# A decoder step in one kernel: one group's shift divided between ACT and POOL, eight squares moved a layer forward, TensorE's idle products in two batches, the last eight rows normed by DVE

## The reference

```
x = layernorm(x + scan(x))             # gates, values = sigmoid, tanh of x @ W.T + b; hidden = gate*hidden + value
x = layernorm(x + ssm(ctx, ctx, x))    # products of context channels, convolved over 128 tokens, times x
x = layernorm(x + routed(x))           # 8 experts: score, best gate, low-rank update
x = layernorm(x + causal_attention(x))
x = layernorm(x + cross_attention(x, ctx))   # quantised weights, self and cross heads
x = layernorm(x + mixture(x))          # 8 experts, the 2 best of each token
```

```
x_diff = x_diff / norm(x_diff)
score  = sum((select_weight . x_diff) ** 2)
gate   = sigmoid(slope * (score - center))        # best expert by the largest gate
out    = (1 - gate) * x + gate * (bias + degen . (update . (x - debias)))
```

## Time and profile before

| | |
|---|---|
| median of 3 runs | 1453.36 us (1452.62 to 1458.38) |
| the profiled execution's own time | 1458.62 us |
| its span, first to last instruction | 1456.9 us |
| mean granted TensorE clock | 0.969 of full |
| busy | PE 93%, DVE 73%, ACT 64%, POOL 60% |
| front block | 0 to 145 us |
| routed block | 145 to 189 us |
| causal attention block | from 189 us |
| last adds landed, rows loaded, normed, stored | 1435.5 us to the end |

### The profile page before, as it was taken

How to read it: one execution, slowest core, us unless ns; L and a number is a source line. 1 busy time by engine, 2 the same in 40 slices (tenths; PEclk the granted TensorE clock), 3 DMA queues, 4 the chain that set the end, 5 groups by cost and what they waited for, 6 DMA issues and landing times. The chain is left out here.

```text
span 1456.9 us, 27654 instructions
## 1 busy us (share of the span) xinstructions
PE 1353.1 (93%) x8289; PEld 1099.2 (75%) x8306; DVE 1060.7 (73%) x2549; ACT 938.7 (64%) x3150; POOL 877.0 (60%) x1052
## 2 busy tenths in 40 slices
PE   9998878895799999999999999999999988999992
PEld 4445656663489999999988888888888856888881
DVE  4898748896788888888988788887788856333332
ACT  3996447775578787888887777777776645222222
POOL 3896127774077676776886756756657622555543
PEclk9999789998999999999999999999999989999996
DMA  9321110000101001010010100100001175333334
GB/s 344 140 116 58 35 45 1 2 2 1 44 2 45 1 1 56 1 49 5 23 62 2 45 1 2 45 1 2 1 1 34 41 249 163 52 52 52 53 47 126
DMA packets 46085, 72.77 MB, mean 50 GB/s; under 512 B 4044, under 2 KB 32660, under 8 KB 43636
## 3 DMA queue, kind: packets, MB, share of 16 engines
q1 hardware_dynamic: 37028, 51.86, 10.5%
q0 software_dynamic: 7488, 10.23, 4.3%
q10 hardware_dynamic: 1424, 8.91, 1.5%
HBM read 50.94 MB, written 20.05 MB: 49 GB/s over the span
## 5 line engine op out<-in xcount | busy, mean ns | idle before, releaser
L1783 ACT ACTIVATE pr_<-ps,neg_ 128x128 f32<-128x128 f32 x512 | 180.9, 365 | 73.4 <-DVE neg_ L1900 72.6
L1841 POOL TENSOR_TENSOR rstd<-var,half 128x6 f32<-128x6 f32 x128 | 172.3, 1346 | 10.1 <-POOL var L1836 0.2
L1800 ACT ACTIVATE y<-ps,invsm 128x128 bf16<-128x128 f32 x512 | 145.5, 368 | 25.7 <-PE ps L1714 25.5
L1836 POOL TENSOR_TENSOR var<-stat,deps 128x6 f32<-128x6 f32 x128 | 25.2, 197 | 224.8 <-DVE stat L1880 224.8
L1852 POOL TENSOR_TENSOR z<-t,m 128x512 fp32r<-128x512 f32 x128 | 148.6, 1161 | 1.7 <-DVE t L1926 1.7
L1696 PE MATMUL ps<-qkt 128*128 128x128 f32 x1024 | 144.5, 284 | 2.3 <-ACT qkt L1775 2.1
L1696 PEld LDWEIGHTS ps<-qkt 128*128 128x128 f32 x1024 | 124.0, 191 | 29.6 <-issue 26.9
L1725 PE MATMUL ps<-phi,z 128*128 128x256 f32 x512 | 137.9, 301 | 0.7 <-POOL z L1852 0.5
L1845 POOL TENSOR_TENSOR pr_<-pr_,rec_ 128x512 f32<-128x512 f32 x128 | 133.2, 1040 | 3.4 <-DVE rec_ L1907 3.4
L1714 PE MATMUL ps<-XT 128*128 128x256 f32 x512 | 132.1, 380 | 0.6 <-ACT XT L1791 0.6
L1725 PE MATMUL ps<-plo,z 128*128 128x256 f32 x512 | 127.6, 282 | 0.0
(11 more groups left out here) (339 smaller groups left out, 3951.2 us busy)
## 6 DMA issues: line engine op xcount, KB each, us to landing
centred<-raw_weights ACTq DMA_DIRECT2D x8, 1024.0 KB, 3.9
w_low<-w_dram SPq DMA_DIRECT2D x8, 1024.0 KB, 10.4
aw_st<-centred SPq DMA_DIRECT2D x7, 1024.0 KB, 5.0
raw_weights<-wself_dram SPq DMA_DIRECT2D x4, 1024.0 KB, 13.8
raw_weights<-wcross_dram SPq DMA_DIRECT2D x4, 1024.0 KB, 14.5
w<-w_dram SPq DMA_DIRECT2D x2, 2048.0 KB, 19.4
aw_rows<-wproj_dram SPq DMA_DIRECT2D x7, 512.0 KB, 4.0
tz<-toep_dram SPq DMA_DIRECT2D x1, 2048.0 KB, 11.7
```

The source lines that it names most:

```text
L1783: ins = act.activation(pr[:, u.par, h, :], bS[:, h * S:(h + 1) * S], ACT.Exp, bias=neg[:, u.par, h:h + 1], accum_out=tot[:, u.par, h:h + 1])
L1800: ins = act.activation(y[:, u.par, h * S:(h + 1) * S], bO[:, h * S:(h + 1) * S], ACT.Copy, scale=invsm[:, head:head + 1])
L1841: pool.tensor_tensor(rstd[:, u.par, 0:6], v, half[:, :], ALU.pow).then_inc(s_rstd, 1)
```

## The change

Four edits.

- **Shift of n0's group 1.** DVE no longer makes it; it waits for rstd and norms its two rows. ACT makes the group's fall behind the first of the four evacuations of the last group, and POOL makes the shift behind rstd, before the last `borders` and `total(2)`. The function is split into `fallen` and `shifted_by_pool`; for the other groups the instructions stay as they were.
- **Eight squares.** The squares of rows 0 to 7 are done by ACT in the front block, behind the keeping of n1's groups 0 and 1 and before its wait for group 2, with the idle `gate` tile as their unused output. xx moves to the weights object that outlives the block. The routed block keeps rows 8 to 15.
- **Idle products.** 7, a wait for Exp (s_ex), 5 more, then the wait for mk (s_mk). Before it was 8 and then the wait for mk.
- **Last rows.** DVE norms all rows of quarters 2 and 3. ACT makes the falls of quarters 0 and 1 ahead of its rows; POOL makes no fall any more, and a shift only for quarters 0 and 1.

```diff
     def deviations_and_shift(self, pool, power, tg):   # split
+    def fallen_by_act(self, act, tg):
+        g = self.group(tg)
+        act.wait_ge(self.means, 4 * tg + 4)
+        act.activation(self.fall[:, g], self.mean_var[:, g, 0], ACT.Copy, scale=-1.0).then_inc(self.falls, 1)
+    def shifted_by_pool(self, pool, tg):
+        g = self.group(tg)
+        pool.wait_ge(self.falls, self.falling.index(tg) + 1)
         pool.wait_ge(self.rstds, tg + 1)
         pool.tensor_tensor(self.shift[:, g], self.fall[:, g], self.rstd[:, g], ALU.mult).then_inc(self.shifts, 1)
...
                 n0.normed_by_act(act, 0)
-                evacuate(3, range(3))
+                evacuate(3, range(1))
+                n0.fallen_by_act(act, 1)
+                evacuate(3, range(1, 3))
                 n0.normed_by_act(act, 1)
...
                 n1.keep_by_act(act, 1, range(CB))
+                routed.squares(act, lambda b: gate[:, b // 4, b // 2 % 2, b % 2 * C:(b % 2 + 1) * C], X, range(B // 2))
                 n1.normed_by_act(act, 2)
...
                 n0.deviations(pool, power, 1)
+                n0.shifted_by_pool(pool, 1)
                 borders(3)
                 total(2)
...
                 scan(2)
-                n0.shifted(dve, 1)
+                dve.wait_ge(n0.rstds, 2)
                 n0.normed_by_dve(dve, 1)
                 scan(3)
...
+    def squares(self, act, out, X, bs):
+        for b in bs:
+            ins = act.activation(out(b), X[:, b, :], ACT.Square, accum_out=self.xx[:, b:b + 1])
+        return ins
...
-        GROUPS, WIDE, DUMMIES = B // 4, 4, 8
+        GROUPS, WIDE, DUMMIES = B // 4, 4, (7, 5)
...
-                for _ in range(DUMMIES):
-                    pe.matmul(weights.projection(ps, 0)[:, 0:W512], ident[:, :], ident[:, :].unsqueeze(1).to_broadcast([P, 4, P]),
-                              start=True, stop=True)
+                for count, s_next in zip(DUMMIES, (s_ex, s_mk)):
+                    for _ in range(count):
+                        pe.matmul(weights.projection(ps, 0)[:, 0:W512], ident[:, :], ident[:, :].unsqueeze(1).to_broadcast([P, 4, P]),
+                                  start=True, stop=True)
+                    pe.wait_ge(s_next, 1)
...
-                for b in range(B):
-                    ins = act.activation(sq[:, b, :], X[:, b, :], ACT.Square, accum_out=xx[:, b:b + 1])
-                ins.then_inc(s_sq, 1)
+                weights.squares(act, lambda b: sq[:, b, :], X, range(B // 2, B)).then_inc(s_sq, 1)
...
-        by_dve = lambda q: range(4 * q, 4 * q + 2) if q >= QUARTERS // 2 else range(0)
+        by_dve = lambda q: quarter_rows(q) if q >= QUARTERS // 2 else range(0)
...
-                for q in range(QUARTERS):
+                for q in range(QUARTERS // 2):
+                    act.wait_ge(s_mean, q + 1)
+                    act.activation(fall[:, quarter(q)], mean_var[:, quarter(q), 0], ACT.Copy, scale=-1.0).then_inc(s_fall, 1)
+                for q in range(QUARTERS // 2):
                     act.wait_ge(s_shift, q + 1)
...
                     pool.wait_ge(s_mean, q + 1)
-                    pool.tensor_scalar(fall[:, quarter(q)], mean_var[:, quarter(q), 0], -1.0, None, ALU.mult).then_inc(s_fall, 1)
...
+                    if by_act(q):
+                        pool.wait_ge(s_rstd, q + 1)
+                        pool.wait_ge(s_fall, q + 1)
+                        pool.tensor_tensor(shift[:, quarter(q)], fall[:, quarter(q)], rstd[:, quarter(q)], ALU.mult
+                                           ).then_inc(s_shift, 1)
```

More of the change, by code:

```diff
@@ L194, with __init__ @@
 class RowNorm:
-    def __init__(self, tag, shared, pairs, ctx, sem, sbuf, X, XT, ps, ident):
-        self.shared, self.pairs, self.X, self.XT, self.ps, self.ident = shared, pairs, X, XT, ps, ident
+    def __init__(self, tag, shared, falling, pairs, ctx, sem, sbuf, X, XT, ps, ident):
+        self.shared, self.falling, self.pairs, self.X, self.XT, self.ps, self.ident = shared, falling, pairs, X, XT, ps, ident
         self.row_stats = sbuf(ctx, tag + "_row_stats", [P, B, 6], F32)
@@ L250, in deviations_and_shift @@
         pool.tensor_scalar(self.fall[:, g], self.mean_var[:, g, 0], -1.0, None, ALU.mult).then_inc(self.falls, 1)
-        self.deviations(pool, power, tg)
-        pool.wait_ge(self.falls, 1 + sum(t not in self.shared for t in range(tg)))
+    def shifted_by_pool(self, pool, tg):
+        g = self.group(tg)
+        pool.wait_ge(self.falls, self.falling.index(tg) + 1)
         pool.wait_ge(self.rstds, tg + 1)
@@ L362, in front_layer @@
         early = sbuf(ctx, "a_early", [P, 1], F32)
-        n0 = RowNorm("n0", (0, 1), ((4, 5), (6, 7), (0, 1), (4, 5)), ctx, sem, sbuf, X, XT, ps, ident)
-        n1 = RowNorm("n1", (2, 3), ((0, 1), (4, 5), (2, 3), (6, 7)), ctx, sem, sbuf, X, XT, ps, ident)
+        n0 = RowNorm("n0", (0, 1), (1, 2, 3), ((4, 5), (6, 7), (0, 1), (4, 5)), ctx, sem, sbuf, X, XT, ps, ident)
+        n1 = RowNorm("n1", (2, 3), (0, 1), ((0, 1), (4, 5), (2, 3), (6, 7)), ctx, sem, sbuf, X, XT, ps, ident)
         centring = Centring(ctx, sem, sbuf)
@@ L582, in _ @@
                     if n == 3:
-                        n0.deviations_and_shift(pool, power, 2)
+                        n0.fallen(pool, 2)
+                        n0.deviations(pool, power, 2)
+                        n0.shifted_by_pool(pool, 2)
                     if n == 7:
-                        n0.deviations_and_shift(pool, power, 3)
+                        n0.fallen(pool, 3)
+                        n0.deviations(pool, power, 3)
+                        n0.shifted_by_pool(pool, 3)
                     if n == 26:
-                        n1.deviations_and_shift(pool, power, 0)
+                        n1.fallen(pool, 0)
+                        n1.deviations(pool, power, 0)
+                        n1.shifted_by_pool(pool, 0)
                     if n == 28:
-                        n1.deviations_and_shift(pool, power, 1)
+                        n1.fallen(pool, 1)
+                        n1.deviations(pool, power, 1)
+                        n1.shifted_by_pool(pool, 1)
                     if n >= 5:
@@ L717, in __init__ @@
         self.pad = sbuf(ctx, "pad", [P, C], F32)
+        self.xx = sbuf(ctx, "xx", [P, B], F32)
         self.loaded, self.filled, self.multiplied, self.summed, self.copied, self.projected = (
@@ L778, in routed_layer @@
         sq = sbuf(ctx, "sq_", [P, B, C], F32)
-        xx = sbuf(ctx, "xx", [P, B], F32)
+        xx = weights.xx
         sc = sbuf(ctx, "sc", [P, B, NE0], F32)
@@ L849, in turn @@
                         mm.then_inc(s_turned, 1)
-                pe.wait_ge(s_mk, 1)
                 for q in range(B // 4):
@@ L2129, in moe_layer @@
         quarter = lambda q: slice(4 * q, 4 * q + 4)
-        by_dve = lambda q: range(4 * q, 4 * q + 2) if q >= QUARTERS // 2 else range(0)
+        quarter_rows = lambda q: range(4 * q, 4 * q + 4)
+        s_power, s_spread = sem("f_power"), sem("f_spread")
+        by_dve = lambda q: quarter_rows(q) if q >= QUARTERS // 2 else range(0)
         by_act = lambda q: range(4 * q + len(by_dve(q)), 4 * q + 4)
@@ L2334, in _ @@
                 skewed(pool, NT // PER, PER, [(gather, 0), (add, ADD)], PEEL)
-                pool.memset(power[:, :], -0.5).then_inc(s_fall, 1)
+                pool.memset(power[:, :], -0.5).then_inc(s_power, 1)
+                pool.wait_ge(s_power, 1)
                 for q in range(QUARTERS):
                     pool.wait_ge(s_mean, q + 1)
-                    pool.tensor_scalar(fall[:, quarter(q)], mean_var[:, quarter(q), 0], -1.0, None, ALU.mult).then_inc(s_fall, 1)
-                    pool.tensor_scalar(spread_[:, quarter(q)], mean_var[:, quarter(q), 1], LN_EPS, None, ALU.add).then_inc(s_fall, 1)
-                    pool.wait_ge(s_fall, 2 * q + 3)
+                    pool.tensor_scalar(spread_[:, quarter(q)], mean_var[:, quarter(q), 1], LN_EPS, None, ALU.add).then_inc(s_spread, 1)
+                    pool.wait_ge(s_spread, q + 1)
                     pool.tensor_tensor(rstd[:, quarter(q)], spread_[:, quarter(q)], power[:, quarter(q)], ALU.pow).then_inc(s_rstd, 1)
-                    pool.wait_ge(s_rstd, q + 1)
-                    pool.tensor_tensor(shift[:, quarter(q)], fall[:, quarter(q)], rstd[:, quarter(q)], ALU.mult
-                                       ).then_inc(s_shift, 1)
+                    if by_act(q):
[3 more added lines that the diff above has]
+                                           ).then_inc(s_shift, 1)
             @block.vector
```

2 lines of the change are left out of this document (1 added, 1 removed).

## The result

The changed kernel took 1445.28 us (median of five runs, 1441.46 to 1448.72) against 1454.91 us of the kernel before on the same chip (1452.62 to 1458.85): a ratio of 0.994, with a 95% interval of 0.9921 to 0.9958. Five more runs on another occasion gave 1444.37 against 1453.92, 0.9937 (0.9922 to 0.9953). The forecast was 1447.3, in a range of 1443.5 to 1453.0. The direction, the order of size and three of four terms held; the fourth, the tail, was ten times larger than forecast, and one step inside the third was wrong. The profiled execution of the changed kernel took 1446.21 us, with a span of 1444.5.

A forecast was written before the change was run, and what follows sets the result against it. Each edit was taken to sit where one engine is waited for, with PE bounding the convolution and stores the tail. Terms 1.1 + 1.95 + 2.95 + 0.15 = 6.15 us, off 1453.36, gave 1447.3 us, range 1443.5 to 1453.0.

The forecast's parts named there:

- the fourth, the tail: Last block: ACT starts sooner and quarter 1 is stored earlier, then 4.5 us of stores follow as before; 0.15 us.
- one step inside the third: Routed block, idle products: the clock falls during the low-rank products, so the last eight transposes run at half; costs 0.65 us.
- scan: Front convolution: without DVE's shift the last scan, held by total(2), and PE's turning back come earlier; 1.1 us.
- squares: Eight squares fit ACT's wait in the front block at no cost, so the routed block's Exp starts earlier; 1.95 us.
- idle products: Routed block: products behind Exp hold PE's clock at full for the transposes and first low-rank products; 2.95 us.
- last rows: Tail: quarter 1 is stored slightly earlier, DVE's sooner finish is covered by the stores; 0.15 us.
- The stores are what is late there, not the rows: Tail: gapless DMA stores, 4.5 us for the last 1.5 MB, set the end, so the term is only 0.15 us.
- The rival of the clock at full: Clock stays at full through the routed block, perhaps into the causal block: 1443.0 to 1446.6 us; chance 0.20.
- The rival of the gain given back: Half clock entering the causal block returns up to 3.65 us (1451), or the longer run time dominates (1452.5); chance 0.19.

The follow-up runs named there:

- e9: Changed kernel with POOL's total(2) held back until the last scan is done, so POOL does nothing beside that scan; 1451.08 us.
- e3: Changed kernel with all sixteen squares in the routed block again; 1447.1 us.
- e6: Changed kernel with nine more idle products in the routed block, ahead of the turns of groups 0 to 3 and behind the last; 1443.13 us.
- e8: Changed kernel with e6's idle products between the turns, and the last quarter's deviation in the tail moved from POOL to ACT and DVE; 1443.63 us, ratio 0.9929.
- e10: Kernel of e8 with two idle products fewer, one ahead of the last turns and one behind them; 1441.89 us, ratio 0.9916.
- e2: Changed kernel with the eight idle products in a row and none behind Exp, as before the change; 1448.66 us.
- e11: The changed kernel run again as it stands, beside e10; 1444.37 us, ratio 0.9937.
- e1: Changed kernel with two more 128x4 powers on POOL behind the tail's last rstd, on a tile nobody reads; 1447.49 us.

## Why the prediction was right, and where not

| step | forecast, us | two executions | that edit alone undone |
|---|---|---|---|
| scan | 1.1 (0 to 1.8) | 1.4 to 1.8 | 1.5 to 1.9 |
| squares | 1.95 (1.6 to 2.09) | 2.05 | 2.05 to Exp, 3.2 in all |
| idle products | 2.95 (0 to 3.6) | 3.0 | 2.4 to 2.5 |
| last rows | 0.15 (0 to 2.03) | 1.53 | 1.52 |
| sum | 6.15 | 8.4 | |

The direction is right and the total is inside the range, but that it came within 2.0 us of the forecast is in part luck. The median fell by 9.6 us, 3.5 more than the sum of 6.15; the median from which the forecast was counted, 1453.36, rose to 1454.91 with two more runs and took 1.6 of that away again. Two slips of arithmetic change nothing: 1453.36 less 6.15 is 1447.2, and a scan that starts at 39.7 and takes 2.34 us ends at 42.04, 1.2 earlier and not 1.15.

**Scan: right, a little small.** `total(2)` started at 36.39 + 0.76 = 37.15 us on the time scale of before (forecast 37.35), ACT's rows at 37.2 (37.3), the last scan at 39.1 (39.0). The scan was then forecast to be held until 39.7 and to run its full 2.34 us from there, to 42.1. It ended at 41.8. The overlap was 0.49 us and the delay 0.34, not the 0.7 of the forecast. PE turned the group back 1.4 us earlier (its first transpose, the ninth of the sixteen that begin at 37.30, at 38.17 instead of 40.31, less 0.76) where 1.1 was forecast, and the first convolution came the same 1.4 earlier. PE ran without a pause from 37.30 to there, so what limited this gain was PE's own work ahead, group 0's transposes, and no longer the rows. The rule cited from the Trainium skill (SBUF — State Buffer, section "Who interferes with whom") is borne out three times: 2.35 and 2.40 us for a shift that starts with POOL's addition, and 2.68 against 2.34 us for a scan with POOL and without (e9). One reading of mine fell short: the 1.00 us of group 0's shift is no free shift either. It ran from 29.80 to 30.80, beside a product of POOL from 29.75 to 30.79. With POOL idle, the same instruction takes 0.13 to 0.16 us, as at the end of the front block in the kernel before:

```profile
139.95 0.16 DVE L259 SCALAR_TENSOR_TENSOR n_shift<-n_mean_var,n_rstd 128x4 f32<-128x4 f32 x1 [0.52 <-POOL n_rstd L245]
```

**Squares: right.** 2.05 instead of 1.95; the weight load behind which the table load waits was itself 0.4 us earlier, so the table did not hold Exp to 155.06. That they cost nothing in front is shown by e3 (11.03 against 11.02), and ACT still had 1.28 us to spare there, as worked out (1.2).

**Idle products: right sum in this pair, one step wrong.** The transposes took 1.94 us, the first residual came 2.5 us earlier relative to the transposes (forecast 1.7 + 0.87 = 2.57), and DVE's pace gained 1.43 where 0.95 was forecast (sixteen residuals in 11.33 us instead of 12.76). Against this the last stretch lost 0.94, not 0.65. The step that failed is "The low-rank products did not bring it back in 12 us of full work, so I expect it to fall during them". It did not: the clock was 1.00 until 166 and fell at 169.9, behind a pause of PE of 1.81 us, with the same slow turns as outcome. All nine traces of the changed kernel and its variants that have this pause of 1.8 us show the clock fall 0.5 to 3.5 us after the pause began; the three in which idle products fill it (e6, e8, e10) show no fall before the causal block. So the cause of the slow turns is shown: it is the pauses. The conclusion that full-clock running would not last there was right by a wrong reason. This is also the correction to how the prediction weighed the Trainium skill (TensorE: Matmul & The Clock Gate, section "What's actually happening"), where activity releases the throttle: e6 and e10 agree, with a clock of 1.00 through the whole routed block, where PE was kept at work, and e2 too, where it came back at 162.4. What the 12 us at half clock of the kernel before were is not explained by that rule, and no run here repeated them. The 3.0 us of this pair, and so the forecast of 2.95, rest on them: in the kernel before the clock was down from 161.1 to 181.6, in e2 from 155.5 to 162.4, and there the same edit was worth 2.4. That the forecast sum was met here is luck to that extent.

**Last rows: mis-sized, ten times too small.** The step is "The stores are what is late there, not the rows", and the value of 0.15 taken from it. Its fact was right, the stores have no gap before and after. Its conclusion was not: last means what the end waits for, and behind the stores SP waited 2.4 us more for the meeting of the engines, by POOL. The edit took four small instructions of fall and two of shift from POOL, and POOL's end moved 1.53 us, and with it the kernel's. The price that decided was that of an instruction nobody had put on the path, because its result (the shift) was not needed late. In SP's waits in the kernel before this was one row, "SPq L2146 <- PEq L2146: 2.4".

**The causal block.** It was forecast to begin 6.0 us earlier, near 183; it began at 181.45, and 7.6 earlier (0.76 of which was there from the start), at half clock as expected, and was not slower for it: 11.06 us against 11.34. The rival of the clock at full did not occur in this kernel, but e10 shows that its price, an estimate of up to 3.65, was about right: 3.55 us less in the first part of the block against the changed kernel's first trace (11.06 to 7.51), and 1.55 against its second (9.06, e11). The rival of the gain given back fell: the medians of the two kernels differ by no less than the edits add up to. Both kernels have their spread of several microseconds from stretches elsewhere.

## What to carry to other kernels

When a kernel ends with a transfer, look at what its issuing engine waits for after the transfer; if it is the meeting of the engines, find the engine whose last instruction keeps a fixed distance to the end, and take work off that one, whether or not its result is wanted. Where a chain leaves PE idle again and again, as the turns did here (1.81, 2.05 and 1.15 us), one or two unused products in each pause can hold its clock, as in e6, e8 and e10, but their number must be fitted to the gap: two too many cost 1.5 us of the routed block here (24.42 against 22.88), more than the clock had cost there, and an edit that moves the neighbouring step changes the right number. Compare two kernels stretch by stretch between shared instructions, since two executions of one kernel can differ by as much as the change is worth.

## What was not expected of the hardware

- POOL ends late. In this last block, in which POOL had issued the indirect DMAs, its part in the block's meeting ended 6.45 us after its last instruction (6.45 or 6.46 in twelve of the thirteen traces, 6.62 in e1), while in the seven other blocks of every trace it ended 0.05 to 0.07 us after it. It is not tied to the stores: POOL's last instruction lay anywhere from 10.6 to 14.6 us behind the load, and the 6.45 stayed. That the indirect DMAs are the reason is a guess from that comparison, and no run tested it.
- A fall of the clock costs more than its own stretch. In e3 a pause of 2.38 us made five products 1.6 us longer, and these delayed the transposes by 1.3 us.
- The same instructions from 200 to 1220 us took 1015 to 1022 us, and the difference goes with the clock in a few places (0.78 to 0.90 between 330 and 400 us).
